# One-pass normalisation on ScalarE in the last stage, a weights' sum on TensorE, relative context scales, and a new order of work in a fused attention and feed-forward kernel

## The reference

```python
x = x + xattn0(layernorm(x), ctx)            # a: both operands rounded to e4m3 grids
x = x + ffn0(layernorm(x), ternary weights)  # b: 512 -> 1408 -> 512
x = x + xattn1(layernorm(x), ctx, mask)      # c: softmax(x ctx^T) ctx
x = x + ffn1(layernorm(x), wg, wu, wd)       # d: 512 -> 2048 -> 512
# layernorm: (x - m) / sqrt(v + eps), no gain or bias
# a: xq = e4m3(xb * 448/amax) * amax/448 in 1x128 blocks; weights alike in 128x128 blocks
# d: h_bitlinear(x, w): Hadamard transform, rounding to 8 bits per token,
#    w to -1, 0, 1 times mean(|w|) over the whole matrix
#    h_bitlinear(silu(h_bitlinear(x, wg)) * h_bitlinear(x, wu), wd)
```

## Time and profile before

| | us | 
|---|---|
| median of 3 runs (lowest to highest) | 739.11 (737.59 to 740.54) |
| the profiled execution, its own time | 739.64 |
| its span | 737.8 |
| busy: TensorE, VectorE, ScalarE, GpSimd | 669.6, 599.8, 408.8, 308.1 |
| granted TensorE clock, mean | 0.988 of full speed |
| stages a and b up to the last chunk's product | 0 to 306 |
| stage c | 333 to 471 |
| stage d with its drain | 471 to 738 |

### The profile page before, as it was taken

The page is one execution under the profiler, slowest core; times in us unless marked ns, Lnnn a source line. Parts: engine busy times, 40 slices in busy tenths (PEclk is TensorE's granted clock), DMA queues, the critical chain, the costliest instruction groups (busy, mean ns, idle before and its releaser), DMA issues.

```text
span 737.8 us, 12353 instructions
## 1 busy us (share of the span) xinstructions
PE 669.6 (91%) x3968; PEld 390.4 (53%) x3968; DVE 599.8 (81%) x1338; ACT 408.8 (55%) x893; POOL 308.1 (42%) x248
## 2 busy tenths in 40 slices
PE   1789799999989999848999999998999999999996
PEld 0466567565848676614444444454455555555554
DVE  7899899999998894215887885679999999999775
ACT  4747576858685564303222222465777677767844
POOL 2023131313323132200000000019999999999980
PEclk9999999999999999969999999999999999999999
DMA  9961242426241524623333420052656746565611
GB/s 220 262 220 22 80 108 65 108 80 123 64 108 40 137 59 139 250 92 115 114 114 117 133 91 1 14 101 58 102 115 122 136 100 126 115 137 120 115 58 43
DMA packets 138307, 79.73 MB, mean 108 GB/s; under 512 B 115730, under 2 KB 117778, under 8 KB 137236
## 3 DMA queue, kind: packets, MB, share of 16 engines
q1 hardware_dynamic: 135348, 74.03, 40.5%
q0 software_dynamic: 2480, 4.33, 3.3%
q10 hardware_dynamic: 432, 0.79, 0.4%
HBM read 51.20 MB, written 4.19 MB: 75 GB/s over the span
## 4 chain that ended last, share of the span: by engine, by line
PE 29%; DVE 29%; issue 26%; ACT 8%; POOL 4%; DMA 2%; POOLq 0%; DVEq 0%; ACTq 0%; SPq 0%
PE ps L1480 12%; PE ps L1495 7%; DVE y_sm L1314 4%; DVE ps L1274 3%; DVE arena L1287 2%; PE ps L1614 2%; PE ps L1442 2%; PE ps L1571 2%; ACT arena L731 2%; DVE arena L1288 2%; DVE arena L1280 2%; POOL arena L461 2%; DVE arena L1033 1%; PE ps L1556 1%; DVE bn_b L842 1%
## 5 line engine op out<-in xcount | busy, mean ns | idle before, releaser
L1480 PE MATMUL ps<-arena 128*128 128x256 f16 x1408 | 160.3, 274 | 12.7 <-DVE arena L1033 6.5
L1480 PEld LDWEIGHTS ps<-arena 128*128 128x128 f16 x1408 | 136.8, 98 | 36.4 <-DVE arena L1033 9.2
L419 POOL TENSOR_TENSOR arena<-arena 128x256 f16<-128x256 f32 x88 | 60.6, 705 | 188.7 <-ACT arena L557 188.7
L1614 PE MATMUL ps<-arena 128*128 128x512 bf16 x512 | 120.9, 380 | 5.5 <-DVE arena L1280 3.8
L460 POOL TENSOR_TENSOR arena<-arena 128x1024 f32<-128x1024 f32 x44 | 103.8, 2359 | 33.7 <-DVE arena L1288 32.2
L461 POOL TENSOR_TENSOR arena<-arena 128x1024 f32<-128x1024 f32 x44 | 106.4, 2417 | 0.0
L1495 PE MATMUL ps<-arena 128*128 128x512 f16 x352 | 80.7, 387 | 1.2 <-POOL arena L419 1.1
L401 POOL TENSOR_TENSOR rstd_a<-ve_a,mhalf 128x1 f32<-128x1 f32 x32 | 19.5, 609 | 148.3 <-DVE ve_a L847 134.6
L1614 PEld LDWEIGHTS ps<-arena 128*128 128x128 bf16 x512 | 47.0, 98 | 61.8 <-DVE arena L1280 12.0
L550 ACT ACTIVATE arena<-ps,gs 128x256 f32<-128x256 f32 x88 | 40.9, 468 | 59.1 <-PE ps L1480 56.4
L739 ACT ACTIVATE arena<-ps 128x512 f16<-128x512 f32 x60 | 35.8, 597 | 47.8 <-DVE ps L1274 46.9
(11 more groups left out here) (144 smaller groups left out, 1161.6 us busy)
## 6 DMA issues: line engine op xcount, KB each, us to landing
arena<-in_ctx_t SPq DMA_DIRECT2D x7, 1024.0 KB, 5.6
arena<-in_wg_t SPq DMA_DIRECT2D x16, 256.0 KB, 3.5
arena<-in_wu_t SPq DMA_DIRECT2D x16, 256.0 KB, 4.0
arena<-in_wd_t SPq DMA_DIRECT2D x16, 256.0 KB, 4.3
arena<-in_ctx_n SPq DMA_DIRECT2D x4, 1024.0 KB, 7.8
arena<-in_wg_t SPq DMA_DIRECT2D x4, 1024.0 KB, 4.9
arena<-in_wu_t SPq DMA_DIRECT2D x4, 1024.0 KB, 4.8
arena<-in_wd_t SPq DMA_DIRECT2D x4, 1024.0 KB, 5.4
```

What stands on the lines that cost most here:

```text
L419: nc.gpsimd.tensor_tensor(hl[:, c, at:at + 2 * P], b_h[n % 4], hh[:, c, at:at + 2 * P], ALU.subtract).then_inc(b_hl_r, 1)
L1480: last = M(bank(n % 2)[:, 2 * P * i:2 * P * i + 2 * P], W[:, b, c * P:c * P + P], part[:, b, at:at + 2 * P], start=(b == 0 and part is xhT ...
L1614: last = M(bank(2 * (n % 2) + i), d_qT[u][:, b, :], W[:, b, D * n:D * n + D], start=(b == 0), stop=(b == KD - 1))
```

## The change

1. The sum of `wsum` over the partitions is a TensorE product with a 128 x 128 matrix of ones (`weight_total`), at the head of the last group, into a PSUM bank that VectorE reads. GpSimd's reduction is gone. `weight_thresholds` stands inside the last group on VectorE.
2. In stage d the normalisation of tile k+2 is one ScalarE activation (`d_normal`, Identity with scale and bias by pointer) with a shift that VectorE computes (`d_center`). It was one VectorE operation.
3. The contexts are scaled back with scales relative to their largest (`crel`), and the tile's scales are multiplied by the largest (`a_back_scales`): 3 small VectorE operations per context, one per tile.
4. The order of work in `b_group` and `d_body` is another on every engine.

```diff
+                V.tensor_reduce(ctop[:, e, 0:1], csd[:, e, :], AX.X, ALU.max).then_inc(c_rel, 1)
+                dve.wait_ge(c_rel, 3 * e + 1)
+                V.reciprocal(ctop[:, e, 1:2], ctop[:, e, 0:1]).then_inc(c_rel, 1)
+                dve.wait_ge(c_rel, 3 * e + 2)
+                V.tensor_scalar(crel[:, e, :], csd[:, e, :], ctop[:, e, 1:2], None, ALU.mult).then_inc(c_rel, 1)
...
+            def a_back_scales(j):
+                u = j % 2
+                dve.wait_ge(c_rel, 3 * (j // 4) + 1)
+                V.tensor_scalar(a_sm[:, u, 3, :], a_sm[:, u, 1, :], ctop[:, j // 4, 0:1], None, ALU.mult).then_inc(a_back_r, 1)
...
-            pool.wait_ge(prep, 1)
-            nc.gpsimd.partition_all_reduce(wtot[:, :], wsum[:, :], P, RADD).then_inc(prep, 1)
...
+            def weight_total():
+                pe.wait_ge(prep, 1)
+                pe.wait_ge(a_add, NT)
+                M(ps[:, 3, 0:3], ones[:, :], wsum[:, :], start=True, stop=True).then_inc(prep, 1)
```

ScalarE in stage b (`b_group`), the head of a group and the end of group 0:

```diff
+                b_silu(g, 0)
                 if g == 0:
                     context_high(0, 0)
                 if g == 1:
                     context_back(1, 2)
                     context_high(1, 2)
...
-                b_silu(g, 0)
...
+                b_high(g, 10)
+                if g == 0:
+                    context_back(1, 1)
+                    context_high(1, 1)
+                if more:
+                    b_normal(n1)
...
-                if g == 0:
-                    context_back(1, 1)
-                    context_high(1, 1)
```

Stage d, ScalarE and VectorE:

```diff
+            def d_normal(j, u):
+                act.wait_ge(d_shift, j - 3)
+                act.wait_ge(d_tp, j - 1)
+                nc.scalar.activation(d_xn[u], tile_of(X, j), ACT.Identity, bias=shift[:, u, :],
+                                     scale=rstd["b"][:, u, :]).then_inc(d_xn_r, 1)
...
                     d_silu(k, u, 3)
                 if front:
                     d_turned(k + 1, w)
+                if ahead:
+                    d_normal(k + 2, u)
                 if whole:
                     d_hi(k, 3)
...
+            def d_center(j, u):
+                dve.wait_ge(st_rstd["d"], j + 1)
+                V.scalar_tensor_tensor(shift[:, u, :], mv["b"][:, u, 0:1], -1.0, rstd["b"][:, u, :],
+                                       ALU.mult, ALU.mult).then_inc(d_shift, 1)
...
+                if mid:
+                    d_hidden(k, u, 1)
                 if whole:
                     d_lo(k, 0)
-                if mid:
-                    d_hidden(k, u, 1)
+                if ahead:
+                    stats("d", k + 2, u)
+                if whole:
+                    d_lo(k, 1)
                 if front:
                     front_scales(k + 1, w)
-                if whole:
-                    d_lo(k, 1)
                 if back:
                     first_stage(k - 1, 0)
                 if mid:
                     d_hidden(k, u, 2)
-                if ahead:
-                    stats("d", k + 2, u)
                 if back:
                     first_stage(k - 1, 1)
                 if whole:
                     d_lo(k, 2)
+                if ahead:
+                    d_center(k + 2, u)
                 if mid:
                     d_hidden(k, u, 3)
                 if out_part:
                     d_residual(k - 4, u)
                 if whole:
                     d_lo(k, 3)
-                if ahead:
-                    d_norm(k + 2, u)
```

257 lines of the change are left out of this document (130 added, 127 removed).

## The result

| | before | after |
|---|---|---|
| median of 5 runs (lowest to highest), us | 738.34 (737.59 to 740.54) | 733.95 (733.34 to 734.45) |
| ratio of the two, 95% interval | | 0.9935 [0.9921, 0.995] |
| profiled execution, its own time / its span | 739.64 / 737.8 | 733.34 / 731.5 |
| busy: TensorE, VectorE, ScalarE, GpSimd | 669.6, 599.8, 408.8, 308.1 | 668.3, 601.9, 417.1, 303.4 |

What follows compares the result with a forecast made beforehand. Three nearly full engines bound most of the kernel, except a hole at stage b's end. Terms -15.1, -1 and +5.6 sum to -10.5 us from 739.64: 729.1, or 728.6 against the median; range 719 to 735.

Steps and rivals of the forecast that it cites:

- part 1: End of stage b: weights' sum on TensorE removes the hole and the lower clock behind it, -15.1 us.
- first-call rule: GpSimd's reduction: cited rule that a freshly loaded kernel's first call costs about 6 us that no instruction shows.
- the period's mechanism: Last stage: ScalarE's chain keeps 3.03 us between hidden products, moved statistics add 1.04; period 15.18 to 15.72 us.
- part 3's body 2: Last stage's body 2 has no back rounding, so it was called better by some 0.3 us.
- the shift fits in: Last stage: VectorE's new 0.15 us shift falls into its 0.9 us idle time before the fourth hidden product.
- part 2: Stage b: relative scales and new order together, -1 us, taken between -8.5 and +4.2.
- 1 us per pair better: Stage b, groups 2 to 5: VectorE waits less for GpSimd's powers, 1 us gained per pair.
- The 1 us of group 0: Stage b, group 0: ScalarE scales a context block back before normalising tile 3, about 1 us worse.
- rival E: Stage b worse by 4.2 us and the last stage by 7, giving 735.2 us; chance 0.10.
- C: End of stage b: the hole stays with GpSimd's first power, slower by 4.2 us, 743.3; chance 0.04.
- D: Last stage: ScalarE's Identity needs table loads in each of 12 tiles, some +19 us, near 748; chance 0.02.
- Rival A: Last stage gets shorter, with TensorE's 14.96 us per tile as floor, -2.4 us, giving 720.6; chance 0.24.

Runs made afterwards that it cites:

- e10: e6 with the one-column shift written as a tensor_scalar taking 1/sigma by pointer; 727.42 us.
- e11: The changed kernel with only the one-column shift rewritten as a tensor_scalar taking 1/sigma by pointer; 732.36 us.
- e6: The changed kernel with the statistics of tile k+2 back behind the last stage's third hidden product, normalisation still on ScalarE; 748.79 us.
- e2: e1 plus the relative context scales, with the orders of stage b and the last stage of the kernel before; 738.03 us.
- e12: e1 with the last stage of e10 (ScalarE normalisation, statistics behind the third hidden product, pointer shift); 724.40 us.
- e1: The kernel before with only the weights' sum over partitions moved to TensorE; 723.66 us.
- e3: The changed kernel with the last stage's orders and VectorE normalisation of the kernel before; 739.32 us.
- e5: e3 with the last stage's normalisation on VectorE written as scalar_tensor_tensor instead of tensor_scalar from body 2 on; 734.53 us.
- e8: e1 with four one-column VectorE instructions put directly ahead of the normalisation in bodies 2 to 13; 751.02 us.

## Why the prediction was right or wrong

**Right: part 1.** -15.1 forecast, -15.76 in the traces, and 723.66 us for it alone, against 723.4 by that term. The lower clock behind the hole went too: the second down product took 4.91 us, not 7.13. One remark beside it was wrong. The forecast put the 7.54 us behind the reduction outside the first-call rule that it cites. The trace of before has a second MODIFY_POOL_CONFIG right there (315.0), so the two stretches look alike, and "6 and not 13 us" does not follow.

**Right: the period's mechanism.** The interval of 3.03 us stayed, with VectorE's wait for the SiLU in it; 15.61 instead of 15.72 us; e10 against e11 shows the statistics as the cause. TensorE was idle 1.53 us in 40 there, 0.6 a tile, where 0.8 was said.

**Wrong: part 3's body 2 and the shift.** The step that failed is the overlap: "the shift fits in", at 0.15 us, and body 2 "is better by some 0.3". The shift has two tensors of SBUF as inputs. In the first tile, which body 2 normalises, it starts 0.07 us behind GpSimd's pass (492.85 and 492.78) and lasts 2.29 us. Forecast -0.3, found +2.2; e11 gives 1.6 us of the median and 1.9 of the head back by its form alone. That the other eleven were short was not foreseen either: they start 0.10 to 0.26 us ahead of a pass, and e6 moved all twelve behind it for 15 us.

**Wrong: part 2.** -1 us forecast, +2.6 in the two traces, the largest miss of the sum. The relative scales cost 1.3 and not about nothing: it seems that VectorE's 28 small operations are not all hidden in a stage where it is busy 33.22 of 35.26 us. (No run separates them from the waits that ScalarE got with them.) That was the row to go by, and its 4.2 us were given as the bound. The order costs 1.8. Its term for groups 2 to 5, "1 us per pair better", came to half in groups 3 and 4 (70.11 to 69.6 us, and 68.9 before the scales), and the last three groups lost 1.1. At the head of group 3 the wait shrank (1.60 to 0.58), but TensorE now waits 0.68 for a subtraction in the down product ahead. The 1 us of group 0 was 1.4 to 1.7.

**The sum.** -15.76 + 2.6 + 2.2 + 4.8 = -6.16, against 6.3 between the profiles. The range held the result, by rival E's side: stage b worse and the last stage at +7. It was given 0.10, and is what happened. That the last stage measured just +7.0 is partly luck: the bound was meant for lost short waits and 0.1 us more per tile, which by its own terms is 11 x (0.54 + 0.3 + 0.1) = 10.3, and the 7.0 came from the first shift. The chances of "same" and "slower" are swapped too: half of E is 0.05, C and D are 0.06.

**Wrong about the rivals.** Rival A had the port lock in its hand, with the 0.2 us of GpSimd's pass as its price. It priced the lock by the side that loses 0.2 us in before, and nobody asked what it costs when the other side loses: 2.3 us a tile. The last stage of before runs with 0.18 us to spare, and e2 shows that with the relative scales alone it goes over. So the worth of the new last stage here is not in the sum of its own instructions. Beside part 1 alone, and in its best form, it brings nothing (e12 against e1: 724.40 and 723.66); beside the other two parts it saves 5.4 us (e3 against the changed kernel).

**Left open.** Why the copy at 559.28 in e2, and the same one in e3 and e5, came 0.28 us late; which instructions of the new orders cost the 1.1 us in the last three groups of stage b; why the clock fell more in some traces than in others behind the head of group 1; what the relative scales cost by VectorE's operations and what by ScalarE's waits.

## What to carry to other kernels

Where VectorE and GpSimd are both nearly full, list the VectorE instructions that can lock with GpSimd, however small: here those were the 512-column tensor_scalar from SBUF to SBUF (0.54 us, where the form with two tensors takes 0.78), and any with two tensors in SBUF. For each, read who starts first and by how much; behind a margin of 0.2 us stood a step of 2.3 us a tile, and an unrelated edit tripped it. Taking the lock away (another engine, or a pointer in place of a second tensor) was worth more here as insurance than its own sum shows.

Take a change apart and run the parts before pricing them together: one of three parts held all the gain, and that part alone beat the whole by 10 us.

## What the runs showed of the hardware that was not expected

- A one-column VectorE instruction with two tensors of SBUF as inputs took 2.11 to 2.29 us in all 12 tiles of e6 beside a GpSimd pass of 2.37 us; with one tensor and a pointer, 0.20 to 0.21 in e10.
- Four one-column instructions per tile cost 27.4 us in the whole kernel (e8 against e1), since each put the normalisation behind GpSimd's pass: 2.28 us a tile.
- Where VectorE's tensor_scalar started 0.2 us ahead, GpSimd's pass was 0.2 us longer (2.57 against 2.36), and beside the two-tensor form 0.45 to 0.5 (2.81 to 2.86, e5); where GpSimd won, VectorE's instruction was up to 2.79 us long. The lock cost 0.2 to 0.5 us or nearly a whole pass.
- GpSimd's sum over partitions cost two idle stretches, 5.63 us ahead of it and 7.54 us behind it, each behind a MODIFY_POOL_CONFIG (308.9 and 315.0); the way back to ordinary instructions was the dearer one. Without the sum, nothing of either is left (e1).
